# Weight chunks turned by DMA instead of TensorE, and a new order for the first loads of a two-layer attention and feed-forward kernel

## What is computed

```python
x = x + matmul(fake_quant(layernorm(x)), fake_quant(ctx))           # 8-bit grid, exact in bf16
x = x + mx_ffn(layernorm(x), w_gate, w_up, w_down)                  # 512 -> 1376 -> 512
#   mx_linear(x, w) = quant_fp6(x) @ quant_fp4(w).T, one shared exponent per block of 32
x = x + attention(layernorm(x), ctx, ctx, mask, wq, wk, wv, wo)     # 32 query heads, 8 key heads of 128, RoPE
x = x + ffn(layernorm(x), gate_w, up_w, down_w)                     # ternary weights, f32
```

## Time and profile before

| what | value |
|---|---|
| median of three runs | 702.44 us |
| the profiled execution | 702.53 us, its span 700.7 us |
| TensorE matmul busy | 668.3 us (95%) |
| VectorE busy | 520.0 us (74%) |
| GpSimd busy | 463.3 us (66%) |
| ScalarE busy | 363.3 us (52%) |
| DMA | 67.27 MB, all on one hardware queue, issued by SyncE |

### The profile page before, as it was taken

How to read it: one execution, slowest core, us unless ns; L and a number is a source line. 1 busy time by engine, 2 the same in 40 slices (tenths; PEclk the granted TensorE clock), 3 DMA queues, 4 the chain that set the end, 5 groups by cost and what they waited for, 6 DMA issues and landing times.

```text
span 700.7 us, 11095 instructions
## 1 busy us (share of the span) xinstructions
PE 668.3 (95%) x3152; PEld 494.0 (70%) x3152; DVE 520.0 (74%) x1046; ACT 363.3 (52%) x686; POOL 463.3 (66%) x407
## 2 busy tenths in 40 slices
PE   6999998899899999999999999999999999799997
PEld 2444443444577788888888888888888877688885
DVE  4999798777668888888888888888888886721122
ACT  2697434533565665666666665665665663211110
POOL 0697426432479878778789788688698478066661
PEclk9999999999999999999999999999999999999999
DMA  9985422140323132141131221221223012013311
GB/s 340 343 293 183 134 87 80 36 155 6 127 71 119 30 106 76 30 134 45 55 110 45 82 83 45 90 75 46 89 75 135 17 31 66 25 46 101 113 56 61
DMA packets 39420, 67.27 MB, mean 96 GB/s; under 512 B 3680, under 2 KB 12000, under 8 KB 38368
## 3 DMA queue, kind: packets, MB, share of 16 engines
q1 hardware_dynamic: 39392, 66.93, 28.9%
HBM read 57.48 MB, written 9.44 MB: 95 GB/s over the span
## 4 chain that ended last, share of the span: by engine, by line
PE 71%; POOL 10%; DVE 8%; issue 7%; ACT 2%; DMA 1%; SPq 0%; POOLq 0%; DVEq 0%; ACTq 0%
PE ps L663 16%; PE ps L665 16%; PE ps L664 16%; PE ps L731 11%; PE ps L696 7%; POOL mx_raw L1104 3%; POOL mx_w L1110 3%; PE ps L584 2%; PE ps L520 1%; DMA X<-in_x 1%; PE ps L536 1%; POOL prob L1161 1%; PE ps L620 1%; DVE mx_amax L1339 1%; DVE stats L1260 1%
## 5 line engine op out<-in xcount | busy, mean ns | idle before, releaser
L1009 ACT ACTIVATE prob<-ps,nmax 128x512 f32<-128x512 f32 x128 | 88.3, 690 | 97.4 <-DVE nmax L1487 97.0
L1161 POOL TENSOR_SCALAR prob<-prob,rinv 128x512 f32<-128x512 f32 x128 | 89.4, 698 | 73.7 <-DVE rinv L1494 73.6
L731 PE MATMUL ps<-xt,wq_sb 128*128 128x512 f32 x384 | 103.2, 393 | 3.8 <-DVE q_cos L1502 2.1
L1020 ACT CAST pT<-ps 128x512 fp32r<-128x512 f32 x128 | 75.1, 587 | 52.8 <-PE ps L696 51.9
L1487 DVE CUSTOM_DVE_ANT_0 ps<-ps,mask_sb 128x512 f32<-128x512 f32 x128 | 87.9, 687 | 6.7 <-PE ps L665 6.3
L1508 DVE TENSOR_TENSOR pT<-ps,pT 128x512 fp32r<-128x512 f32 x128 | 86.3, 674 | 3.0 <-ACT pT L1020 2.0
L731 PEld LDWEIGHTS ps<-xt,wq_sb 128*128 128x128 f32 x384 | 71.6, 188 | 22.0 <-issue 4.6
L696 PE MATMUL ps<-idf,prob 128*128 128x128 f32 x512 | 76.7, 272 | 0.4 <-POOL prob L1161 0.3
L696 PEld LDWEIGHTS ps<-idf,prob 128*128 128x128 f32 x512 | 63.8, 141 | 17.3 <-POOL prob L1161 1.6
L520 PE MATMUL ps<-ctxT,wk_sb 128*128 128x512 f32 x128 | 60.5, 613 | 6.5 <-DMA ctxT<-in_ctx_cols 6.5
L1104 POOL TENSOR_TENSOR mx_raw<-mx_raw,mx_r 128x2048 f32<-128x2048 f32 (+1 forms) x9 | 30.2, 3354 | 53.7 <-DVE mx_r L1347 53.7
(11 more groups left out here) (177 smaller groups left out, 1587.9 us busy)
## 6 DMA issues: line engine op xcount, KB each, us to landing
mx_raw<-in_mxw SPq DMA_DIRECT2D x8, 1024.0 KB, 5.5
wq_raw<-in_wq SPq DMA_DIRECT2D x32, 256.0 KB, 3.2
wo_raw<-in_wo SPq DMA_DIRECT2D x32, 256.0 KB, 2.7
v_scr<-v_st SPq DMA_DIRECT2D x16, 256.0 KB, 2.5
kr<-k_scr SPq DMA_DIRECT2D x16, 256.0 KB, 2.9
vr<-v_scr SPq DMA_DIRECT2D x16, 256.0 KB, 3.4
k_scr<-k_st SPq DMA_DIRECT2D x14, 256.0 KB, 2.1
kr_swp<-k_scr SPq DMA_DIRECT2D x28, 128.0 KB, 3.3
```

The source lines that it names most:

```text
L731: last = mm(query_bank(H), wq_sb[:, par, l, k], xt[:, r, k], start=(n == 0), stop=(n == 11))
L1009: nc.scalar.activation(prob[:, j], bank(j % 2), ACT.Exp, bias=nmax[:, j:j + 1], scale=-1.0, accum_out=rsum[:, j:j + 1]).then_inc(exps, 1)
L1020: copy(pT[:, v % 2, 0, :, i * P:(i + 1) * P], bank(2 + i % 2).rearrange("p (k c) -> p k c", k=4)).then_inc(ph_ready, 1)
L1161: nc.gpsimd.tensor_scalar(prob[:, i], prob[:, i], rinv[:, i:i + 1], 1.0, ALU.mult, ALU.mult).then_inc(probs, 1)
```

## The change

Parts of the diff, in the order of the streams:

1. **Turning by DMA.** `mx_turn` (132 TensorE transposes), `mx_keep` (17 ScalarE copies), `turn_quantised(0)` and its `keep_quantised(0)` go. SyncE issues one transposing DMA for each chunk, and four for the quantised rows. `scale_out(i)` now waits for the turning of chunk i - 2 (`WT_in`). TensorE waits for `WT_in` of chunks 0 to 5 ahead of the gate and up products and of 6 to 8 ahead of the first down product.
2. **First loads.** x comes first; the first half of the context columns and of wv come in four slices each; TensorE starts with the four value units of step 0, slice by slice; both units of key head 0 follow.
3. **GpSimd.** It computes the reciprocals of the scales, scales in halves (two instructions for a chunk), and `key_rotate(0)` and `key_rotate(1)` stand behind `scale_out(0)` and `scale_out(1)`.
4. **VectorE.** The fp6 chain has two instructions less, the root chain for a single column has 7 instead of 9.
5. **One late key less.** Unit ("k", 5, 1) goes into step 7; the other four keep their places.

```diff
 STEPS = (
-    ([("v", 0, 0), ("v", 1, 0), ("v", 2, 0), ("v", 3, 0)], [("k", 0, 1)]),
+    ([("v", 0, 0), ("v", 1, 0), ("v", 2, 0), ("v", 3, 0)], [("k", 0, 0), ("k", 0, 1)]),
...
-    ([("v", 7, 1), ("k", 5, 0)], []),
+    ([("v", 7, 1), ("k", 5, 0), ("k", 5, 1)], []),
 )
-LATE_KEYS = ((5, 1), (6, 0), (6, 1), (7, 0), (7, 1))
+LATE_KEYS = ((6, 0), (6, 1), (7, 0), (7, 1))
...
+            def slice_load(k):
+                sp.dma_start(ctxT[:, k, 0:CTX], ctx_cols[k * P:(k + 1) * P, 0:CTX]).then_inc(ctxT0_in[k], 16)
+                sp.dma_start(wv_sb[:, k, 0:512], wv[k * P:(k + 1) * P, 0:512]).then_inc(wv0_in[k], 16)
...
+            def chunk_turn(i):
+                n = 1 if i == NFULL else MXT
+                sp.wait_ge(mx_ready, 2 * NFULL + 1 if i == NFULL else 2 * i + 2)
+                sp.dma_start(WT[:, MXT * i:MXT * i + n].rearrange("p t (k r) -> p (t k) r", r=P), mx_w[:, i % 2, 0:n * D],
+                             transpose=True).then_inc(WT_in[i], 16)
+
+            def rows_turn():
+                sp.wait_ge(q1_ready, NT)
+                for t in range(NT):
+                    sp.dma_start(q1T[:, :, t * P:(t + 1) * P], q1[:, t], transpose=True).then_inc(q1T_in, 16)
+
+            sp.dma_start(X[:], x.rearrange("(t p) d -> p t d", p=P)).then_inc(x_in, 16)
+            slice_load(0)
+            sp.dma_start(sc[:], scalars).then_inc(sc_in, 16)
+            slice_load(1)
+            mx_load(0)
+            slice_load(2)
+            slice_load(3)
+            mx_load(1)
             k_load(0)
...
+            mx_load(2)
             sp.dma_start(idf[:], ident).then_inc(id_in, 16)
             sp.dma_start(ropeK[:], rope_k).then_inc(rk_in, 16)
+            ctx_load(0)
+            sp.dma_start(wv_sb[:, :, 512:1024], ...
             k_load(1)
             stores(STEPS[0][0])
             mx_load(NRAW)
             ctx_load(1)
...
-                stores(STEPS[i][0] + STEPS[i][1])
+                stores(STEPS[i][0])
+                if i == Q_AT:
+                    rows_turn()
+                chunk_turn(i - 1)
+                stores(STEPS[i][1])
             k_load(6)
-            sp.wait_ge(mx_turned, 2 * NFULL + 1)
+            for i in range(NFULL - 1, NCH):
+                chunk_turn(i)
+            for i in range(NFULL - 1, NCH):
+                sp.wait_ge(WT_in[i], 16)
...
+            def first_values():
+                units = STEPS[0][0]
+                for k in range(KD):
+                    pe.wait_ge(ctxT0_in[k], 16)
+                    pe.wait_ge(wv0_in[k], 16)
+                    for unit in units:
...
+            first_values()
             for i in range(NFULL):
-                project_context(STEPS[i][0])
...
+                if i > 0:
+                    project_context(STEPS[i][0])
+                project_context(STEPS[i][1])
+                if i == L0_AT - 1:
                     pe.wait_ge(consts_ready, 2)
+                    pe.wait_ge(q1T_in, 16 * NT)
                     attention0(0)
...
             gate_up(0)
-            mx_turn(NFULL - 2, 0)
-            mx_turn(NFULL - 2, 1)
-            gate_up_slice(1, 0)
-            mx_turn(NFULL - 1, 0)
-            gate_up_slice(1, 1)
-            mx_turn(NFULL - 1, 1)
-            late_keys(0, range(0, 2))
-            gate_up_slice(1, 2)
-            mx_turn(NFULL, 0)
-            pe.wait_ge(mx_kept, 2 * NFULL + 1)
+            gate_up(1)
+            pe.wait_ge(mx_free, 2 * NFULL + 1)
             turn_inter(0)
             gate_up(2)
             down(0)
-            late_keys(0, range(2, 4))
...
-            swap(0)
+            rows_scale()
+            mx_lift(0, 0)
+            mx_lift(0, 1)
             copy_values(0, 0)
             copy_values(1, 0)
...
             def scale_in(i):
+                m, p = width(i) // BLK, i % NRAW
+                pool.wait_ge(mx_expo, i + 1)
+                ts(mx_r[:, p, 0:m].bitcast(I32), mx_e[:, p, 0:m].bitcast(I32), -1.0, -(2.0 ** 24), ALU.mult, ALU.add).then_inc(mx_scale, 1)
                 pool.wait_ge(mx_scale, i + 1)
+                for cols in halves(i):
+                    n, lo = (cols.stop - cols.start) // BLK, cols.start // BLK
+                    tt(blocks(mx_raw[:, p, cols]), blocks(mx_raw[:, p, cols]), over(mx_r[:, p, lo:lo + n], n), ALU.mult).then_inc(mx_scaled, 1)
 
             def scale_out(i):
                 pool.wait_ge(mx_rounded, i + 1)
-                after(pool, mx_turned, 2 * (i - 1))
+                if i >= 2:
+                    pool.wait_ge(WT_in[i - 2], 16)
...
-            key_rotate(0)
 
             for i in range(NFULL):
                 if i + 2 <= NFULL:
...
                 scale_out(i)
-                if i == 0:
-                    key_rotate(1)
+                if i < 2:
+                    key_rotate(i)
...
             def fp6(src, n, turn):
-                chain(f6s, ts(f6_amax[:, 0:m], f6_amax[:, 0:m], 2.0 ** -100, None, ALU.max))
                 chain(f6s, ts(f6_amax[:, 0:m].bitcast(U32), f6_amax[:, 0:m].bitcast(U32), EXP_MASK, None, ALU.bitwise_and))
-                chain(f6s, ts(f6_r[:, 0:m].bitcast(I32), f6_amax[:, 0:m].bitcast(I32), -1.0, float(0x7F000000), ALU.mult, ALU.add))
-                chain(f6s, ts(f6_r[:, 0:m], f6_r[:, 0:m], 2.0 ** -4, None, ALU.mult))
+                chain(f6s, ts(e, f6_amax[:, 0:m], 2.0 ** -100, 2.0 ** 4, ALU.max, ALU.mult))
+                chain(f6s, ts(f6_r[:, 0:m].bitcast(I32), e.bitcast(I32), -1.0, float(0x7F000000), ALU.mult, ALU.add))
```

More of the change, by code:

```diff
@@ L216, in build @@
         ctx_in = [sem(f"ctx_in{i}") for i in range(2)]
[L217 to L218 removed]
+        ctxT0_in = [sem(f"ctxT0_in{k}") for k in range(KD)]
+        wv0_in = [sem(f"wv0_in{k}") for k in range(KD)]
+        ctxT1_in, wv1_in = sem("ctxT1_in"), sem("wv1_in")
         rk_in = sem("rk_in")
@@ L276, in build @@
         for i in range(NFULL):
-            rotation += STEPS[i][0] + STEPS[i][1]
-            if i == Q_AT:
-                rotation += [("q", 0, 0), ("q", 0, 1)]
+            rotation += STEPS[i][0][1 if i == 0 else 0:] + STEPS[i][1]
             if i == L0_AT - 1:
@@ L287, in rotating @@
         def rotating(unit):
+            if unit == ("v", 0, 0):
+                return 0
             return ROTATE[place[unit] % len(ROTATE)]
-        def mx_bank(i, h):
-            return 2 if i in (NFULL - 2, NFULL - 1) and h == 1 else 0
         def keys_out(i, b):
@@ L505, in attention0 @@
                     last.then_inc(l0_sums, 1)
[L507 to L514, removed]
-                                                   mx_w[:, i % 2, h * HALF + lo:h * HALF + lo + P], idb[:])
-                last.then_inc(mx_turned, 1)
             def key_part(i, b, n, parts):
@@ L569, in _ @@
             pe.wait_ge(q1_ready, NT + 1)
-            turn_quantised(1)
-            pe.wait_ge(q1T_ready, 4)
-            pe.wait_ge(*keys_out(5, 0))
+            turn_quantised()
+            pe.wait_ge(q1T_ready, 2)
+            pe.wait_ge(*keys_out(5, 1))
             pe.wait_ge(mx_free, 2 * NFULL)
-            pe.wait_ge(mx_kept, 12)
+            for i in range(2 * NI // MXT + 1):
+                pe.wait_ge(WT_in[i], 16)
             slices = [(0, 4), (4, 8), (8, 11)]
@@ L615, in down @@
                 pe.wait_ge(intT_ready, t + 1)
-                if t == 1:
-                    pe.wait_ge(*keys_out(*LATE_KEYS[0]))
+                if t == 0:
+                    for i in range(2 * NI // MXT + 1, NCH):
+                        pe.wait_ge(WT_in[i], 16)
                 after(pe, ffn0_done, t - 1)
@@ L1276, in standardise @@
                 chain(ln, ts(r.bitcast(I32), var.bitcast(I32), -0.5, float(0x5F3759DF), ALU.mult, ALU.add))
-                for _ in range(3):
+                if hi - lo == 1:
+                    for three in (3.0, 3.0 * 2.0 ** 2, 3.0 * 2.0 ** 8):
+                        chain(ln, ts(step, r, var, r, ALU.mult, ALU.mult))
+                        chain(ln, stt(r, step, -three, r, ALU.add, ALU.mult))
+                    chain(ln, ts(r, r, -(2.0 ** -13), None, ALU.mult))
+                for _ in range(0 if hi - lo == 1 else 3):
                     chain(ln, stt(step, r, -0.5, r, ALU.mult, ALU.mult))
@@ L1407, in _ @@
                     dve.wait_ge(ln_ready, 2 * NT)
-                    fp6(rows(xhat[:]), NT * D)
+                    fp6(rows(xhat[:]), NT * D, 0)
                     fp6_clip(NT * D, [])
```

177 lines of the change are left out of this document (68 added, 109 removed).

## The result

The changed kernel takes **707.38 us** (median of 4 runs, 706.85 to 708.0) beside 701.74 us for the kernel before (4 runs, 700.72 to 703.03): a ratio of 1.0077, with a 95% interval of 1.0062 to 1.0093. The forecast was 698.7 us, faster than before; the change is slower by 0.8%. The profiled execution took 707.5 us with a span of 705.4 us, where the span before was 700.7.

The account below looks back on a forecast made before the run. TensorE was taken to bound stage one, VectorE and its loads following closely; in stage two VectorE and TensorE alternate. 702.5 - 1.8 (stage one) - 1.9 (stage two) = 698.8, against the median 698.7 us; range 691.5 to 707.5.

Parts of the forecast that it names:

- five turnings' issues: On SyncE behind the stores: four row turnings and chunk 0's, priced as plain issues, 5 x 0.45 us.
- its landing: Chunk 5's load was to land 5.5 us after its issue, at 63.1 us.
- from there to the read: VectorE from chunk 5's landing to its first read of the attention: 9.6 us, so the read at 72.7 us.
- stage two: Alternating VectorE and TensorE slices: 1.2 us from the fp6 chain, 0.7 from the half late key gone, 1.9 us won.
- The rotation: GpSimd's second key rotation, now behind `scale_in(3)` and `scale_out(1)`, was to end at 52.8 us, some 4.1 for its instructions.
- GpSimd's wait for `WT_in`: Listed as a sign that the forecast is wrong: GpSimd waiting for a chunk's turning; no time was given.
- Rival B: Transposing issues hold SyncE: 1.8 us each adds 6.7 us before chunk 5's load, 705.4 us; chance 0.21.
- Rival D: TensorE restarts slowly behind the first attention and before tile 1's last slice, 2 us each: 702.7 us; 0.17 with small delays.
- Rival C: Slow turning transfers: two half megabytes at 16.1 us each put 32 us ahead of chunk 5, 727 us; chance 0.04.
- Rival A: Chunk 5 arrives before VectorE wants it, TensorE bounds stage one: 692.1 us; 0.22 including results between it and forecast.
- The chains: Stage two on VectorE: shorter fp6 chain saves 0.3 us for each of four tiles, 1.2 us; root chain nothing.
- The stretch behind stage two: From stage two's first row transposes to the end: unchanged; a difference would refute the frame of the sum.

Follow-up runs that it names:

- experiment 11: Changed kernel with chunk 5's load directly behind the two stores that wait for the rotation, ahead of the turnings: 703.74 us, ratio 1.0034.
- Experiments 1: Changed kernel with chunk 5's load issued between the two stores of key head 0, before SyncE's wait for the second rotation: 702.68 us, ratio 1.0015.
- experiment 12: Changed kernel with the rows' turnings and chunk 0's turning ahead of the two stores, chunk 5's load left behind them: 701.82 us, ratio 1.0004.
- Experiment 3: Changed kernel with plain copies of the same sizes in place of the transposing DMAs, so nothing is turned: 705.35 us, ratio 1.0054.
- experiment 2: Changed kernel with the rows' turnings, chunk 0's turning and chunk 5's load ahead of SyncE's wait for the second rotation: 694.03 us, ratio 0.9895.
- experiment 7: Changed kernel with 63 unread bf16 products in TensorE's waits, 55 in the middle of the first attention, 8 behind it: 706.14 us, ratio 1.0072.
- 10: Kernel of experiment 2 with 25 unread bf16 products put into TensorE's waits: 694.14 us, ratio 0.9894.
- experiment 5: Kernel of experiment 2 with the fp6 chain and the root chain of the kernel before: 696.36 us, ratio 0.9921.
- experiment 6: Kernel of experiment 2 with the fifth late key back in its old places in stage two: 696.35 us, ratio 0.992.
- its repeat: Kernel of experiment 2 measured again, unchanged: 694.76 us, ratio 0.9894.

## Why the prediction was wrong

By its steps; "after" is the trace of the changed kernel:

| step | forecast | after |
|---|---|---|
| first product | 7.2 us | 7.79 |
| first attention begins | 64.3 | 64.69 |
| SyncE past the stores | 52.8 | 54.96 |
| five turnings' issues | 2.25 | 7.79 |
| load 5 issued | 57.6 | 65.81 |
| its landing | 5.5 | 6.9 |
| from there to the read | 9.6 | 8.8 |
| attention read | 72.7 | 81.53 |
| sixteen products behind it | 7.03 | 9.04 |
| gate and up | 120.0 | 130.86 |
| stage two | -1.9 | -2.9 |
| rest | 0 | -1.5 |

**The step that failed is the one on SyncE**, above all its term of 5 x 0.45 us for the turnings' issues. The chain that I followed was the one that decided, link for link: put the measured 72.7 us of the load into "from there to the read" and it gives 82.3; measured 81.5. What failed is how I priced its beginning. Load 5 left 8.2 us late: 5.5 from the turnings' issues, which I took at the price of a plain issue (0.45 us), and they cost 1.38 us for each row tile and 2.29 for the chunk; 2.2 from the rotation; 0.5 from two small issues. The landing added 1.4, for I took the median of the eight loads of before, 5.5 us, and that median is 7.9 after. "I take the plain price, since these are issues of the same queue" was the sentence at fault: that the queue is the same says nothing of another kind of instruction. Summed up, the load's 8.2 us and the landing's 1.4, less 0.8 between it and the read, and 2.0 for TensorE's slow restart, which had no term, make 10.8 of the 10.9 us by which gate and up came late.

**The rotation** ended 1.8 us later than counted: GpSimd finished `scale_out(1)` 0.7 us later (a chunk in halves took 3.78 us where an instruction of the same size took 3.64, and the reciprocals took 0.24 us more), and the three instructions took 5.2 us instead of 4.1.

**A wait that I didn't price.** I named GpSimd's wait for `WT_in` as a sign of error but gave it no term. By my own times chunk 0's turning was to be issued near 57 us, and GpSimd was to be ready for chunk 2 just as early (52.8 us and 3.8 for the scaling in), so the turning's whole landing was a wait. It took 7.9 us, and only the still later load hid it. By my own times it would have been hidden too: issued by 57 us at the plain price and landed 4.5 us later, chunk 0's turning would have let GpSimd finish chunk 2 near 65.3 us, when VectorE was to be through the peaks of chunk 5 (63.1 + 2.3). So it is the dear issues behind the stores that made it a second limit. And putting the load right is not enough: in experiment 11 it left at 55.12 us, earlier than the forecast's 57.6, and the time was 703.7 us all the same. Experiments 1, 11 and 12 take the two waits apart: the early load alone gives 4.3 us back, the load just behind the stores 3.0, the early turnings alone 5.1, early load and turnings together 12.8. The two waits hide each other here, so the single gains (4.3 and 5.1) add up to less than that of both.

**Rival B** (the turnings hold SyncE, 0.21) is what happened, though not at its price. It was to decide from 1.65 us an issue; the mean was 1.56, and the time was 2 us above B's 705.4, because the rotation, the landing and the restart were added to it. Experiment 3 puts what the price beside a plain copy's is worth at 1.6 us in the total and 3.2 us at the gate and up products; experiment 2 shows that a still higher price is harmless ahead of the stores. So B's cause, told rightly, is the order: five issues behind a wait, and a load behind both.

**Rival D** (TensorE cools) was right in price for one of its two places: 2.0 us (9.04 against 7.03) behind the attention; the slice behind the 2.94 us wait ran at 1.47 us, at full pace. The Trainium skill's "TensorE: Matmul & The Clock Gate", section on the HAM clock gate, says that an idle array falls to half clock; the granted clock of 0.73 in a stretch with waits of 14.1 us agrees. In the total this part isn't separable (experiments 7 and 10).

**Rival C** (slow transfers) is refuted. Chunk 0's turning of 16 tiles landed 4.5 us after its issue. "VectorE: DVE Perf Modes" of the Trainium skill, section "The three transpose paths", gives 1309 ns for one 128 x 128 by DMA; here the whole of the landing is 0.28 us for each tile. The Trainium skill's "Advanced Engine Details and Errata", section "X-Bar Transpose (TRN2)", calls such DMAs as fast as regular ones. In landing the runs don't bear that out fully (median 4.4 us for the nine chunks, beside 3.0 for the plain copies of experiment 3), in issue not at all: 2.07 us in the median beside 0.47.

**Rival A** (the load is not late) did not occur in the changed kernel; experiment 2 made it come true by another order: TensorE waited only 1.22 us for VectorE, and the time is 694.0 beside A's 692.1.

**Stage two** won 2.9 us. The chains are worth 1.25 (forecast 1.2, experiment 5). The late key's absence from stage two is worth 0.7 there (experiment 6: 52.94 us, less 1.56 of slow pace, beside 50.65), as forecast, though its unit costs the same in stage one. The other 0.9 us show up by tile 1's last slice: it starts 11.90 us after gate and up with the old chains (experiment 5) and 13.13 us in the kernel before, where transposes of chunks and half a late key stood between the slices. The half key costs nothing at that place (11.61 us in experiment 6 without the slow pace, 11.59 in experiment 2), so the transposes are left as the cause; that wasn't tried by itself.

**The stretch behind stage two** was to be unchanged, and a difference was to refute the sum. It is 1.5 us shorter (523.9 us instead of 525.4). Over all fourteen traces here it ranges from 523.2 to 525.5 us (524.8 and 524.9 in the kernel of 2 and its repeat), so no effect of the change can be told there, and the sum isn't refuted by it.

**Open.** Turning back on TensorE with everything else as changed was not tried, so what the turning by DMA is worth in itself isn't known. Nor is it settled why a load on this queue needs 6.9 us there; with plain copies it needed 7.0, and 5.9 where it was issued ahead of them (experiment 11). Nor was the changed order of the first loads tried by itself.

## What to carry to other kernels

An in-order issuing queue is a place where waits add up: before a step is moved to it, write down every instruction behind each of its waits, with the time by which someone needs it, and put the urgent ones ahead of the wait. Experiment 2 moved three calls (the rows' turnings, chunk 0's turning and load 5) and turned 0.8% slower into 1.1% faster (0.9894, 0.9876 to 0.9911, in the repeat). A kind of instruction that the trace doesn't hold has no price there; where the bounds are 0.45 and 3.11 us and five such issues stand ahead of a load on the path, the forecast must say which order makes the price irrelevant.

## What was new about the hardware

- In the changed kernel the issue of a transposing DMA kept SyncE for 1.26 to 1.58 us for a tile of 128 x 512 bf16 (1.40 to 2.28 in experiment 2, issued from 34.7 us on), and for 1.67 us at the least and 2.07 in the median for a chunk of 128 x 2048:

```profile
L358 SPq DMA_TRANSPOSE WT<-mx_w x9: 1673/2067/6592, 62.2 to 138.3; - x9
```

- A chunk's turning whose issue began 1.5 to 1.8 us after that of a 1 MB load took 5.97 us (experiment 6) to 8.47 us (experiment 2) to issue. Plain copies in such places, 1.9 and 2.1 us behind the load's issue, took 0.50 and 1.82 us (experiment 3).

- Behind a wait TensorE ran at either pace. In the profiled executions sixteen key products took 7.13 us behind waits of 0.87, 0.93, 1.22 and 1.65 us, and 8.83 to 9.81 behind waits of 1.95, 2.18, 2.60, 8.35 and 9.39 us, or of 1.8 to 2.3 us shortly after one of 2.6 to 12.3; the granted clock from 60 to 80 us was 1.00 in the first group and 0.73 to 0.91 in the second. The slice behind 2.93 or 2.94 us took 1.47 or 1.48 us in eight traces, 2.05 in experiment 7 and 2.74 in experiment 11.
- Executions of one kernel differ by 3 us, and the slow ones are those with the lower mean granted clock (experiment 12), so differences of 1 to 2 us between variants need the granted clock beside them.
